# Graph attention on one core: flagged rows' slots dropped before the gather, and a reordered tail

## The reference

```python
h = jnp.maximum(_layernorm(x, axis=-1), 0.0)
s_i = h @ attn[:d];  s_j = h @ attn[d:]
e = leaky_relu(s_i + s_j.T, negative_slope=0.2)
e = e + where(adj > 0, 0.0, -1e9)
x = x + softmax(e, axis=1) @ h
```

## Time and profile before

| | |
|---|---|
| time, median of 3 runs | 822.92 us |
| span of the profiled execution, first to last instruction | 819.9 us |
| around the span (median minus span) | 3.0 us |
| DMA | 301.59 MB, mean 368 GB/s |
| busy share: DVE, ACT, POOL, PE | 75%, 65%, 62%, 46% |

### The profile page before, as it was taken

How to read it: one execution, slowest core, us unless ns; L and a number is a source line. 1 busy time by engine, 2 the same in 40 slices (tenths; PEclk the granted TensorE clock), 3 DMA queues, 4 the chain that set the end, 5 groups by cost and what they waited for, 6 DMA issues and landing times.

```text
span 819.9 us, 6412 instructions
## 1 busy us (share of the span) xinstructions
PE 379.5 (46%) x1378; PEld 171.4 (21%) x1378; DVE 615.3 (75%) x2028; ACT 534.3 (65%) x410; POOL 505.0 (62%) x526
## 2 busy tenths in 40 slices
PE   1546334444444344344343434444434546653765
PEld 1322011111111011111111101111111215431654
DVE  6898298677768667797778666697689799897831
ACT  4975676676676666766766666676676677764620
POOL 6720777755457767665547677555557667655771
PEclk9776665555555555555555555655555556766768
DMA  8999999999999999999999999999999999981210
GB/s 341 402 411 415 392 404 408 406 414 413 409 407 410 408 405 410 406 410 410 412 406 407 408 406 407 411 410 413 412 413 409 408 411 407 409 348 43 53 37 4
DMA packets 39719, 301.59 MB, mean 368 GB/s; under 512 B 10682, under 2 KB 17149, under 8 KB 22272
## 3 DMA queue, kind: packets, MB, share of 16 engines
q1 hardware_dynamic: 24032, 277.04, 83.1%
q0 software_dynamic: 15360, 23.88, 8.5%
q10 hardware_dynamic: 288, 0.26, 0.1%
HBM read 303.76 MB, written 8.98 MB: 381 GB/s over the span
## 4 chain that ended last, share of the span: by engine, by line
DMA 76%; issue 11%; DVE 5%; ACT 4%; PE 3%; POOL 0%; DVEq 0%; ACTq 0%
DMA adj_ring<-in_adj_dram 75%; ACT sign_ring L613 3%; PE words L1442 2%; DVE one_hot L724 1%; ACT h_all L625 1%; PE words L1406 1%; DMA x_all<-in_x_dram 1%; PE words L1366 0%; DVE cand L769 0%; DVE adj_ring L1142 0%; DVE adj_ring L1138 0%; DVE adj_ring L1146 0%; PE words L1516 0%; POOL out_dram L562 0%; ACT terms L620 0%
## 5 line engine op out<-in xcount | busy, mean ns | idle before, releaser
L613 ACT ACTIVATE sign_ring<-adj_ring,half_neg 128x4096 fp8e3<-128x4096 int32 x128 | 474.9, 3710 | 217.1 <-DMA adj_ring<-in_adj_dram 215.4
L521 POOL DMA_INDIRECT near<-h_table,near_id x384 | 391.8, 1020 | 235.4 <-issue 122.8
L1366 PE MATMUL words<-sign_ring,pack_w 128*128 128x512 bf16 x512 | 225.2, 592 | 354.8 <-ACT sign_ring L613 354.8
L769 DVE MAX8 cand<-words 128x8 f32<-128x256 f32 x256 | 90.9, 417 | 115.4 <-PE words L1366 115.4
L1366 PEld LDWEIGHTS words<-sign_ring,pack_w 128*128 128x128 bf16 x512 | 55.0, 127 | 521.9 <-ACT sign_ring L613 451.6
L954 DVE TENSOR_REDUCE sums<-terms 128x128 f32<-128x1024 f32 x58 | 112.2, 1934 | 2.0
L532 POOL DMA_INDIRECT near_m<-h_table,id_m x64 | 64.5, 1008 | 19.5 <-issue 19.2
L949 DVE TENSOR_TENSOR terms<-near,weight 128x512 f32<-128x512 f32 (+1 forms) x87 | 73.4, 871 | 0.0
L1357 PE MATMUL words<-place,place_w 128*128 128x512 bf16 x128 | 62.1, 586 | 3.6 <-DVE key L861 3.6
L1392 PEld LDWEIGHTS listing<-cand,one_hot 128*128 128x128 f32 x128 | 33.6, 321 | 10.9 <-issue 7.7
L1347 PE MATMUL listing<-h_all 128*1 128x128 f32 x128 | 19.1, 322 | 22.8 <-ACT h_all L625 22.8
(11 more groups left out here) (271 smaller groups left out, 524.3 us busy)
## 6 DMA issues: line engine op xcount, KB each, us to landing
adj_ring<-in_adj_dram SPq DMA_DIRECT2D x128, 2048.0 KB, 24.6
near<-h_table,near_id POOLq DMA_INDIRECT x384, 6.4
h_table<-h_all POOLq DMA_DIRECT2D x4, 1056.0 KB, 14.7
x_all<-in_x_dram SPq DMA_DIRECT2D x4, 1024.0 KB, 9.4
out_dram<-x_all SPq DMA_DIRECT2D x30, 128.0 KB, 23.9
near_m<-h_table,id_m POOLq DMA_INDIRECT x64, 6.4
out_dram<-x_all ACTq DMA_DIRECT2D x2, 128.0 KB, 2.5
adj_ring<-h_table SPq DMA_DIRECT2D x1, 132.0 KB, 2.6
```

The costliest lines, as they stand in the source:

```text
L521: pool.indirect_dma_start(out=near[:, p % RING, k, :], out_offset=None, in_=table, in_offset=bass.IndirectOffsetOnAxis(ap=near_id[:, p % I ...
L613: nc.scalar.activation(bytes_of, adj_ring[:, n % HALVES, :].rearrange("p (d r i) -> p d r i", r=2, i=WORDS), ACT.Sign, bias=half_neg[:, :] ...
L769: last = nc.vector.max(out=cand[:, p % 2, t % 2, 8 * q:8 * q + 8], in_=words[t % 3][:, q * PART:(q + 1) * PART])
L1366: last = nc.tensor.matmul(at[:, k * BANK:(k + 1) * BANK], pack_w[:, d, :], twins[:, o + k * BANK:o + (k + 1) * BANK], start=False, stop=(d ...
```

## The change

`DROPPING` is 30.

1. **Pairs 0 to 29.** `flag_pair` runs before the slot numbers are made. A new `keep` is 0 for a flagged row, and `drop_listed` multiplies the row's best codes by it, so all its slots count as unused in `place_slots`. Its share of `flag_pair` that counts flags is now `count_pair`.
2. **Pair 31.** The first tile is decoded and its four own slots gathered apart (`find_first`), before the second tile is there (`find_second`). `key_pair(30)` and `weigh_pair(29)` also come before the second tile.
3. **DVE's tail order**: `find_deep(3)` before `lone_compact`, `score_pair(31)` before `lone_part`, `lone_end` before `score_deep`.
4. **TensorE**: `mix_pair(29)` before `rank_pair(31)`. The loop's `value_load` before `mix_pair(31)`, and the loop waits for pair 30 closed, not 31.
5. **ACT**: `close_pair(29)` before `exp_pair(30)`. `exp_pair(31)` and the `value_load` before `exp_lone`.
6. **Second lone sum**: the 64 products go to four groups of 32 output partitions in turn, ACT copies the four sums out, and one more matmul adds them.
7. **POOL's last stores**: lone first, then the deep one. The final waits on them are on SP.

```diff
             def find_pair(p):
 ...
                 nc.vector.tensor_tensor(invalid[:, p % IDS, :], best_f[:, :], floor_f[:, :], ALU.is_lt) \
                     .then_inc(find, 1)
                 dve.wait_ge(find, f + 9)
-                nc.vector.tensor_tensor(best[:, 1, :], best[:, 1, :], best[:, 3, ::-1], ALU.max).then_inc(find, 1)
-                dve.wait_ge(find, f + 10)
-                nc.vector.tensor_scalar(power[:, :], best_f[:, 0:SLOTS].bitcast(i32), EXPONENT, None,
-                                        ALU.bitwise_and).then_inc(find, 1)
 ...
-                nc.vector.tensor_tensor(near_id[:, p % IDS, :], offset[:, :], unused[:, :], ALU.add) \
-                    .then_inc(near_id_ready, 1)
                 nc.vector.tensor_reduce(missing[:, :], invalid[:, p % IDS, :].rearrange("p (a k) -> p a k", a=2),
                                         AX.X, ALU.add).then_inc(find, 1)
+            def drop_listed(p):
+                dve.wait_ge(flagging, FLAG * p + FLAG_KEEP)
+                nc.vector.tensor_tensor(
+                    best_f[:, :].rearrange("p (a k) -> p a k", a=2), best_f[:, :].rearrange("p (a k) -> p a k", a=2),
+                    keep[:, :].unsqueeze(2).broadcast_to([P, 2, 2 * OWN]), ALU.mult).then_inc(find, 1)
+            def place_pair(p):
+                f = found(p) + FIND_CODES - (p >= DROPPING)
+                dve.wait_ge(find, f + 1)
+                nc.vector.tensor_tensor(best[:, 1, :], best[:, 1, :], best[:, 3, ::-1], ALU.max).then_inc(find, 1)
+                dve.wait_ge(find, f + 2)
+                place_slots(p, f + 2, slice(0, SLOTS))
             def flag_pair(p):
 ...
+                nc.vector.tensor_scalar(keep[:, :], listable[:, ts], 0.0, None, ALU.is_ge).then_inc(flagging, 1)
 ...
-            for p in range(1, PAIRS):
+            for p in range(1, PAIRS - 1):
 ...
                 find_pair(p)
+                if p < DROPPING:
+                    flag_pair(p)
+                    drop_listed(p)
+                place_pair(p)
+                for g in mixes:
+                    weigh_mix(g)
+                    add_row(g, 0)
+                if p >= DROPPING:
+                    flag_pair(p)
+                count_pair(p)
 ...
+            p = PAIRS - 1
+            lone_begin(p)
+            max_tile(2 * p)
+            score_pair(BODY)
+            find_first(p)
+            key_pair(p - 1)
+            weigh_pair(BODY)
+            max_tile(2 * p + 1)
+            find_second(p)
+            flag_pair(p)
+            count_pair(p)
+            key_pair(p)
+            lone_mark(LAST)
+            score_pair(BODY + 1)
+            find_deep(SEGS - 1)
+            weigh_pair(BODY + 1)
+            lone_compact(LAST)
+            mark_severe()
+            lone_bounds(LAST)
+            size_loop()
+            dve.sem_inc(far_used, 1)
             score_pair(BODY + 2)
+            for c in range(LONE_PARTS[LAST]):
+                lone_part(LAST, c)
             weigh_pair(BODY + 2)
 ...
+            lone_end(LAST)
             score_deep(SEGS - 1)
             add_deep(SEGS - 1)
-            lone_end(LAST)
@@ gpsimd
+                if p == PAIRS - 1:
+                    gather_pair(p, range(OWN))
+                    gather_pair(p, range(OWN, SLOTS))
 ...
+            store_lone(LAST)
             store_m(SEGS - 1)
-            store_lone(LAST)
-            pool.wait_ge(stored_m, 16 * SEGS)
-            pool.wait_ge(lone_stored[0], 16)
-            pool.wait_ge(lone_stored[LAST], 16)
@@ sync
+            sp.wait_ge(stored_m, 16 * SEGS)
+            sp.wait_ge(lone_stored[0], 16)
+            sp.wait_ge(lone_stored[LAST], 16)
@@ scalar
             write_diagonals(BODY)
+            close_pair(BODY)
             exp_pair(BODY + 1)
-            close_pair(BODY)
             write_diagonals(BODY + 1)
             close_pair(BODY + 1)
             store_pair(BODY + 1)
+            exp_pair(BODY + 2)
+            act.wait_ge(sizes_ready, 2)
+            tiles = act.value_load(far_tiles[0:1, 0:1], min_val=1, max_val=TILES)
+            parts = act.value_load(far_parts[0:1, 0:1], min_val=1, max_val=DC)
             for c in range(LONE_PARTS[LAST]):
                 exp_lone(LAST, c)
-            exp_pair(BODY + 2)
             write_diagonals(BODY + 2)
 ...
+            act.wait_ge(lone_fourths_out, 1)
+            nc.scalar.activation(lone_quarters, lone_fourths, ACT.Copy).then_inc(lone_quarters_ready, 1)
             exp_m(SEGS - 1)
@@ tensor
+            def lone_matmuls_last():
+                e = LONE_CAP[LAST]
+                part = lone_p[LAST][0]
+                pe.wait_ge(lone_exp[LAST], 1)
+                for k in range(TILES):
+                    q = k % QUARTERS
+                    last = nc.tensor.matmul(lone_fourths[32 * q:32 * q + e, :], part[:, k * e:(k + 1) * e],
+                                            h_all[:, k, 0:ONE + 1], start=(k < QUARTERS), stop=(k >= TILES - QUARTERS),
+                                            tile_position=(0, 32 * q))
+                last.then_inc(lone_fourths_out, 1)
+                pe.wait_ge(lone_fold_ready, 1)
+                pe.wait_ge(lone_quarters_ready, 1)
+                nc.tensor.matmul(lone_sum[LAST], lone_fold[:, :], lone_quarters, start=True, stop=True) \
+                    .then_inc(lone_summed[LAST], 1)
 ...
-            rank_pair(PAIRS - 1)
             pe.wait_ge(maxed, TILES)
+            mix_pair(BODY)
+            rank_pair(PAIRS - 1)
             pe.wait_ge(keyed, PAIRS)
-            lone_ranks(LAST)
             list_pair(PAIRS - 1)
-            mix_pair(BODY)
+            lone_ranks(LAST)
             lone_spreads(LAST)
 ...
             mix_pair(BODY + 1)
-            mix_pair(BODY + 2)
-            pe.wait_ge(pair_mixed, PAIRS)
             pe.wait_ge(sizes_ready, 2)
             tiles = pe.value_load(far_tiles[0:1, 0:1], min_val=1, max_val=TILES)
             parts = pe.value_load(far_parts[0:1, 0:1], min_val=1, max_val=DC)
+            mix_pair(BODY + 2)
+            pe.wait_ge(pair_mixed, PAIRS - 1)
```

More of the change, by code:

```diff
@@ L161, in graph_attention_kernel @@
         lacking = sb("lacking", [P, 2], fp32)
+        keep = sb("keep", [P, 2], fp32)
         curve = sb("curve", [P, 2], fp32)
@@ L259, in graph_attention_kernel @@
         assert early_taken[0] <= DEAD * D
+        lone_quarters = end(ONE + 1, fp32)
         far_h = end(DB * COLS, fp32).rearrange("p (k c) -> p k c", k=DB)
@@ L288, in graph_attention_kernel @@
         lone_spread = [rank[:, 448:448 + LONE_CAP[0]], words[0][:, BANK:BANK + LONE_CAP[1]]]
-        lone_sum = [rank[0:LONE_CAP[0], 260:260 + ONE + 1], words[2][0:LONE_CAP[1], BANK:BANK + ONE + 1]]
+        lone_sum = [rank[0:LONE_CAP[0], 260:260 + ONE + 1], words[1][0:LONE_CAP[1], BANK + 32:BANK + 32 + ONE + 1]]
+        lone_fourths = words[2][:, BANK:BANK + ONE + 1]
         x_in = [sem(f"x_in{i}") for i in range(XC)]
@@ L514, in _, with gather_pair @@
             pool.sem_inc(far_free, 1)
-            def gather_pair(p):
-                pool.wait_ge(near_id_ready, p + 1)
+            def gather_pair(p, slots=range(SLOTS)):
+                pool.wait_ge(near_id_ready, p + 1 + (slots[-1] == SLOTS - 1 and p == PAIRS - 1))
                 if p >= RING:
                     pool.wait_ge(pair_mixed, p - RING + 1)
-                for k in range(SLOTS):
+                for k in slots:
                     pool.indirect_dma_start(
@@ L824, in find_pair, with find_first @@
                                         AX.X, ALU.add).then_inc(find, 1)
+            def find_first(p):
+                f = found(p)
+                e = p % 2
+                dve.wait_ge(maxed, 2 * p + 1)
+                nc.vector.tensor_scalar(cand_i[:, 0, :], cand[:, e, 0, 0:CAND], 1.0 / UNIT, 3.0 * EACH,
+                                        ALU.mult, ALU.add).then_inc(find, 1)
+                nc.vector.tensor_copy(cand[:, e, :, CAND:REC], h_all[:, 2 * p:2 * p + 2, SI:ROW + 1]).then_inc(find, 1)
+                dve.wait_ge(find, f + 1)
+                nc.vector.tensor_scalar(cand_i[:, 0, :], cand_i[:, 0, :], EACH, None, ALU.bitwise_xor).then_inc(find, 1)
+                dve.wait_ge(find, f + 3)
+                nc.vector.tensor_tensor(
+                    codes[:, 0, :, :], cand_i[:, 0, :].unsqueeze(2).broadcast_to([P, CAND, CHUNKS]),
+                    code_mask[:, :].unsqueeze(1).broadcast_to([P, CAND, CHUNKS]), ALU.bitwise_and).then_inc(find, 1)
+                nc.vector.tensor_copy(cand[:, e, 0, 0:CAND], cand_i[:, 0, :]).then_inc(find, 1)
+                dve.wait_ge(find, f + 4)
+                nc.vector.max(out=best_f[:, 0:8], in_=codes[:, 0, :, :].rearrange("p w c -> p (w c)")) \
+                    .then_inc(find, 1)
+                dve.wait_ge(find, f + 6)
+                place_slots(p, f + 6, slice(0, OWN))
@@ L1215, in _ @@
             find_pair(0)
+            flag_pair(0)
+            drop_listed(0)
+            place_pair(0)
             dve.wait_ge(extreme_spread, 1)
```

(27 more changed lines are left out.)

107 lines of the change are left out of this document (79 added, 28 removed).

## The result

The changed kernel takes 815.21 us (median of 4 runs, 813.67 to 816.79), the kernel before beside it 822.89 (822.07 to 823.05, 4 runs). The ratio on record is 0.9915, 95% interval 0.9902 to 0.9928: 0.85% faster. (The two medians alone divide to 0.9907, inside the interval.) The profiled execution took 815.03 us, of which 813.2 are its span.

What follows compares the result with a forecast made beforehand. Bytes were taken to pace the stream, and three chains of waits the tail. Span 819.9 - 3.3 (bytes) + 0.2 (DVE lag) + 0.2 (last issue) - 1.3 (drain) = 815.7; with 3.0 around it 818.7, range 814.0 to 822.4.

Steps and rivals of the forecast that it cites:

- rival A: Tail better than forecast: pair 29 mixed before the flags, high clock in pairs 30 and 31, or shorter sum; 815, 17%.
- The stream: Loads and gathers, paced by bytes: dropped slots take 1.38 MB out, worth 3.3 us, bounds 0 and 4.0.
- 0.2 us of DVE lag: DVE at the stream's last tile: the drop's added operations were charged 0.2 us of delay there.
- Rival B: The stream keeps its length, through few dropped rows on late engines or DVE becoming the bound: 822.0, no change, 12%.
- First tile apart: Pair 31's gathers on POOL: first four out at 752.3, last issue ends at 767.6 instead of 773.95.
- hide nothing more: Deep gathers on POOL: starting them earlier gains nothing, as the deep mix runs behind the lone sum.
- Order on TensorE: mix_pair(29) ahead of pair 31's rank stalls DVE: key of pair 31 at 761.1, against 760.06 before.
- ACT as the new wait: Late severe count, close_pair(30) and value_load delay pair 31: diagonals at 781.5 against 777.81, lone sum 1.35 us later.
- Lone sum: Second lone sum on TensorE in four column groups: 6.5 us instead of 15.46, plus 1.0 for copy and folding product.
- the upper bound: Second lone sum on TensorE: 15.46 us if products in the four column groups do not overlap at all.
- Order behind the loop: lone_end ahead of score_deep on DVE: deep chain of 7.1 us runs behind the lone sum, last issue 811.15 against 810.92.
- The end: POOL's closing drain starts 0.1 us after the last issue's end, not 1.4: 1.3 us saved, bounds 0 and 1.4.

Runs made afterwards that it cites:

- experiment 1: The changed kernel with keep always 1, so no slot is dropped but DVE runs the same instructions: 814.33 us, 0.9949 of the kernel before.
- experiment 2: The changed kernel without drop_listed and with all slot numbers made before the flags, keep still worked out: 812.72 us, 0.9935 of the kernel before.
- Experiment 11: The changed kernel with all 12 gathers of pair 31 issued together behind its second tile: 814.28 us, 0.9906 of the kernel before.
- Experiment 6: The changed kernel with pair 31's rank and the lone ranks ahead of mix_pair(29) on TensorE, exp_pair(30) ahead of close_pair(29) on ACT: 809.52 us, 0.9882.
- Experiment 7: The changed kernel with exp_pair(31) and the value_load ahead of close_pair(30), and pair 31's diagonals ahead of exp_lone, on ACT: 810.33 us, 0.9890.
- experiment 3: The changed kernel with all 64 products of the second lone sum in one column group and one sum: 823.94 us, 1.0061 of the kernel before.
- experiment 9: The changed kernel with deep mix before lone_end, rank before mix_pair(29), pair 31's exponentials before close_pair(30), and exp_m(3) before the lone sums' copy: 807.44 us, 0.9836.
- experiment 10: The changed kernel with four orders changed on DVE, TensorE and ACT, and the folding matrix built just before the first max_tile: 807.96 us, 0.9829.
- experiment 12: The changed kernel with the final waits for the three stores on POOL instead of SP: 815.06 us, 0.9929 of the kernel before.
- experiment 4: The changed kernel with score_deep and add_deep ahead of lone_end on DVE, and the deep store first on POOL: 809.96 us, 0.9899.

## Why the prediction was right

It forecast 818.7 us, 0.5% faster, in a range of 814.0 to 822.4. Measured were 815.2. That is faster, 0.85% for 0.5, and in the range, but below the forecast's own range (816.5 to 820.8) and at the 815 of rival A, which had 17%. The stalls, the order and what came last were as forecast. Four terms were mis-sized: the stream's gain by 0.6 us (too hopeful) and three costs by 1.2 to 1.6 us (too dear). Two of these three are what A named, the high clock in the mixing of pair 31 and a lone sum of 4 to 5 us.

**The stream, 3.3 us forecast.** The bytes were right (1.38 MB counted, 1.37 measured), the price too high: the last MAX8 came 2.53 us earlier (752.74 to 750.21), and experiment 1 gives 2.0 for the bytes alone. The 0.2 us of DVE lag did not show, as the last MAX8 still waited 1.26 us for its words. 2.5 for 3.3 less 0.2 is 0.6 us short. Rival B fell with experiment 1.

**First tile apart.** The first deep gather went out at 766.86. From the last MAX8 that is 16.7 us against 15.2 forecast: POOL was not free in time and began with pair 31 at 751.01, 0.8 us behind the last MAX8, where I had it 0.4 ahead. The issues of pair 30 show why. Its first in the kernel before, then its first and fourth in the kernel after (timeline of POOL):

```profile
736.62 1.02 POOL L521 DMA_INDIRECT near<-h_table,near_id  x1 [4.59 <-DVE near_id L821]
...
733.96 2.02 POOL L539 DMA_INDIRECT near<-h_table,near_id  x1 [3.87 <-DVE near_id L912]
738.90 1.38 POOL L539 DMA_INDIRECT near<-h_table,near_id  x1 [0.30 <-issue]
```

They begin as far ahead of the last MAX8 as before (16.2 and 16.1 us), but two of them took 1.4 us longer than before, 2.02 and 1.38 for 1.02 and 1.00. Why these two issues were longer stays open. It isn't the drop, as experiments 1 and 2 have the same two (2.02 and 1.38). Experiment 11 shows that it did not matter, as the prediction said ("hide nothing more").

**Order on TensorE, and ACT as the new wait.** The two stalls were placed and sized right, the rank at 8.4 us and the diagonals at 28.7 behind the last MAX8. Experiments 6 and 7 took each away and got time back, 2.35 and 1.5 us, so both were on the path, though for less than expected there. The mixing of pair 31 and the loop together were 1.2 us shorter than forecast. The window of the kernel after in which this mixing begins:

```profile
778.00:780.00 2.00, 0.68 (x5) 0.68 (x5) 0.42 (x3) 2.00 (x5) 1.39 (x3) 1.00 0.47 138
```

The granted clock is 1.00 as the mixing begins, and 0.73 and 0.50 in the next two windows of 2 us. Its first half, at 779.32, took 3.01 us, where before, at 0.50, it took 3.79. The good match at the key is partly luck: over the traces that step alone takes 7.2 to 8.8 us. So is the match at the diagonals, which start 26.9 to 29.4 us after the last MAX8 in the traces with this order.

**Lone sum, the term that was sized worst.** 6.5 us forecast, 4.89 measured, 0.038 for each product and load. The start at the low clock, for which I put 0.9 us on top of 5.6, did come. Windows of the kernel after, L1561 alone (us, busy of PE and PEld, PEclk, DMA share, GB/s):

```profile
792.00:794.00 2.00, 1.89 (x36) 1.50 (x40) 0.50 0.01 0
795.00:796.00 1.00, 1.00 (x48) 0.94 (x40) 1.00 0.00 0
```

In the first, at 0.50, 36 products begin in 1.89 us, 0.052 each. In the second, at 1.00, they begin 0.0275 us apart (the 48 take in those still under way at its edges). So what was mis-sized is the price of a product, 0.044. The row L1426 that it came from ran at 1.00 and in one column group, and was 0.0165 us too dear for that clock. At one clock the groups gain more than 15.5 / 4.9 = 3.2 times, too: in experiment 3 the products begin 0.110 us apart at 1.00, which is 4.0 times as far. Of the two readings of the Trainium skill, "TensorE: Matmul & The Clock Gate", Part 3, weighed there, the one on column groups held, with these 4.0 times for four groups where the page has 2.38 for three. By the other, that a weight load passes a running product only if the row group differs, the sum should have come nearer to the upper bound, and it did not, with all four groups in the same rows.

**Order behind the loop.** 0.92 for copy and fold (1.0 forecast), 0.53 for `lone_end` (0.65), 7.14 from L1109 to the store (7.1). The deep mix did move behind the lone sum, and experiments 9 and 10 show what the orders that the change fixed cost together: with the four orders changed the same work ends 0.7 to 0.8% earlier.

**The end.** 1.4 us saved for 1.3 forecast, and experiment 12 puts it down to the engine on which the last waits stand.

**The sum again.** The forecast span of 815.7 plus 0.6 (stream), less 3.0 (lone start 1.3, lone sum 1.6, the rest 0.1), less 0.1 (end) is 813.2, the measured span. I had put 3.0 us around the span, the median of one set of runs less the span of another execution. Where both are known for one execution it is 1.8 (815.03 less 813.2). That is the last 1.2 us.

The gain has two halves. Without the drop (experiments 1 and 2) the changed kernel is 0.5 to 0.65% faster than before, and the drop adds 0.2 to 0.4%.

## What to carry to other kernels

When one long step in a tail gets short, list for each engine what is queued behind it and what comes last now: here 10.6 us left TensorE, and some 6 us more came only when TensorE, DVE, ACT and POOL were reordered to match (experiment 9). Move a step on all engines that it touches or not at all; experiment 4 got a third of its gain because its partner on ACT stayed behind. Judge reorderings of a microsecond by stretches of the trace from a common event, and by several traces, since the lone sum of the same code started up to 2.9 us later in one trace than in another. When a price is taken from the nearest row, read the granted clock of that row as well.

## What the hardware showed beyond expectation

- Products of 128x16 weights (128x129 values, fp32) in four column groups, with a sum for each group, began 0.0275 us apart at a granted clock of 1.00, with all four groups on the same rows. In one group and one sum it was 0.110 at the same clock (experiment 3). With the part at the low clock they took 0.038 and 0.121 each on average.
- A gathered row left out was worth about 0.7 of the time of its bytes, with as many packets in the queue (15,360): 1.6 us for 0.95 MB, where 408 GB/s make 2.3.
- POOL's closing drain ends 6.4 us after the last indirect issue or, where POOL waits for the landing first, 6.4 us after that. So the landing (807.8 in the kernel after, whose drain ends at 812.9) fits inside it.
- The key of pair 31 came 7.2 to 8.8 us after the last MAX8 in traces with the same order of work in between, with the granted clock of the mixing beside it rising sooner or later (0.55 or 1.00 in one window of 2 us).
